# The expert layer: first products from rounded parts, biases in 128 rows, both batches in one program, weights fetched beside the attention

## The chip, the cores and the metric

The kernel is one program on one core of a Trainium2 chip. The core has a tensor engine (PE), a vector engine (DVE), a scalar engine (ACT), a general engine (POOL) and a sync engine that issues most DMAs (SP). The metric is the time of one execution on the device in microseconds; the median of several executions counts.

## The reference, cut to what matters

x has two batches of 2048 tokens of 128 numbers. Four layers follow each other, each with a residual and a layer norm: a state space mixer, a layer quantised to four bits, an attention with 16 heads, and the experts. Only the last one changes in what it computes:

```
flat = hidden.reshape(T, 128)
weights = the two largest of softmax(flat @ router_w + router_b), zero elsewhere   # 8 experts
shared  = gelu(flat @ sw1 + sb1) @ sw2 + sb2                                       # 128 -> 256 -> 128
h1      = gelu(einsum('td,edh->teh', flat, rw1) + rb1)                             # all 8 experts, 256 wide
expert  = einsum('teh,ehd->ted', h1, rw2) + rb2
out     = layernorm(x + shared + einsum('ted,te->td', expert, weights))
```

Every expert is computed for every token, in fp32.

## The kernel before

`build` runs three phases one after the other: `phase1` (mixer and quantised layer), `phase2` (attention) and `phase3` (experts). Each phase reads its input from DRAM and writes it back (`x_mid`), and each goes over the two batches with a hardware loop, `nc.Fori`. Inside a phase the engines run programs of their own, written out in blocks and tied together by semaphores; every block ends with a barrier of all engines, which also clears the semaphores. The order of the work on each engine is the order of its instructions; no planner is involved.

**Attention.** Per batch: `attention_input` (load, layer norm, transpose; its SP program also fetches the weights of the first two pairs of heads), `attention_first` (keys, queries and values of the first pair, and the maxima of its scores), `attention_pairs` (the long part, 1024 units over both batches) and `attention_output`. Keys and queries are split into a main part in the rounded type fp32r and a rest, `rest = exact - main`. A score is the sum of three fp32r products (main x main, main x rest, rest x main, L1176) and a fourth that subtracts the row's maximum. These products are over 64 rows and come in pairs, one for each head of a pair, on the two halves of the array. The maxima come from L957, also fp32r; the product of probabilities and values, L1187, is fp32.

**Experts.** `phase3` has a first block that fetches the weights with 17 DMAs, nine from SP and eight from ACT (L1461, L1467), waits for them, and makes the table `order`. Then the loop over the batches begins. A batch is 4 chunks (`CHUNKS`) of 512 tokens, a chunk has 9 steps (`ALL`): 8 experts and the shared one. For step k:

- `up(k)` on PE (L1547): two products of 128x512, fp32. The profile shows each fp32 product as two records.
- ACT applies gelu with the bias of the first layer (L1603), twice per step, into `hid`.
- `down(k)` on PE (L1563): for each of four groups of 128 tokens two products with 128 columns. In the ninth step each group begins with one more product, `weightT` (the routing weights, transposed, 9 rows) times `down_b` (the 9 second biases, 9 rows), L1561.
- DVE multiplies by the token's routing weight into `part` (L1684), and POOL adds it to `mixed` (L1715).

PE issues `up(k + 1)` ahead of `down(k)`; both have two sets of PSUM banks. The preparation of the next chunk is spread over the steps of this one: the weights' transpose at step 2, x's transpose at step 3 (L1530) with ACT's copy at step 4 (L1590), the router's products at step 5 (L1538) followed by DVE's `bias`, and exp (L1594) and `choose` (about 17 small DVE operations, L1635 to L1651) at step 7. The layer norm of a chunk runs during the steps of the next: `centre`, `square_act`, `variance`, POOL's power, `scale`, and SP stores the result. In the first chunk of a batch, the load, transpose, router and `choose` come one after the other before the first step; after the last chunk the norm and the store stand alone.

Of the kernel before, what the change touches and what calls it, by code (L numbers as in the profile page):

```python
# [23 lines left out]
P = 128  # L24
# [36 lines left out]
class Phase:  # L61


    def __init__(self, nc):
        self.nc, self.ctx, self.sems = nc, ExitStack(), []
# [8 lines left out]
    def sbuf(self, name, shape, dt=F32):  # L74
        return self.ctx.enter_context(self.nc.sbuf_tensor(name, shape, dt))

    def sem(self, name):
        s = self.ctx.enter_context(self.nc.semaphore(name))
        self.sems.append(s)
        return s  # L80
# [105 lines left out]
def build(nc, ins, out):  # L186

    x_mid = [nc.dram_tensor(f"x_mid_{i}", (BATCH, SEQ, D), F32, kind="Internal").ap() for i in range(2)]
    with Phase(nc) as ph:
# [5 lines left out]
        made, copied = ph.sem("made"), ph.sem("copied")  # L195
# [17 lines left out]
        phase2(nc, ins, x_mid[0], x_mid[1], **shared)  # L213
        phase3(nc, ins, x_mid[1], out, **shared)
# [596 lines left out]
def phase2(nc, ins, x_in, x_out, ident, ident_bf, ones, exponent, psum):  # L811


    with Phase(nc) as ph:
# [28 lines left out]
        common = {k: x for k, x in locals().items() if k not in ("nc", "x_in", "x_out", "ins", "ph")}  # L843

        with Phase(nc) as su:
            zero_one = su.sbuf("zero_one", [P, 2])
            loaded, filled, constants, step = (su.sem(s) for s in ("loaded", "filled", "constants", "step"))
# [23 lines left out]
        with nc.Fori(0, BATCH) as b:  # L871
            attention_input(nc, ins, x_in, b, common)
            attention_first(nc, common)
            attention_pairs(nc, ins, common)
            attention_output(nc, x_in, x_out, b, common)


def attention_input(nc, ins, x_in, b, m):
# [3 lines left out]
    with Phase(nc) as su:  # L882
# [120 lines left out]
def attention_first(nc, m):  # L1003
# [3 lines left out]
    with Phase(nc) as su:  # L1007
# [13 lines left out]
        with nc.Block() as block:  # L1021
            @block.tensor
# [67 lines left out]
def attention_pairs(nc, ins, m):  # L1090
# [26 lines left out]
    with Phase(nc) as su:  # L1117
# [245 lines left out]
def attention_output(nc, x_in, x_out, b, m):  # L1363
# [3 lines left out]
    with Phase(nc) as su:  # L1367
# [62 lines left out]
def phase3(nc, ins, x_in, out, ident, ident_bf, ones, exponent, psum):  # L1430
# [3 lines left out]
    ALL = EXPERTS + 1  # L1434
    with Phase(nc) as ph:
        up_w = ph.sbuf("up_w", [P, ALL, HID])
        down_w = ph.sbuf("down_w", [P, ALL, HH, D])
        up_b = ph.sbuf("up_b", [P, ALL, HH])
        down_b = ph.sbuf("down_b", [ALL, D])
        router_w = ph.sbuf("router_w", [P, EXPERTS])  # L1440
        router_b = ph.sbuf("router_b", [P, EXPERTS])
        order = ph.sbuf("order", [P, EXPERTS])
        stat = ph.sbuf("stat3", [P, 4, TILES])
        with Phase(nc) as su:
            loaded, made = su.sem("loaded"), su.sem("order_made")
            order_i = su.sbuf("order_i", [P, EXPERTS], mybir.dt.int32)
            loads = [
                (up_w[:, 0:EXPERTS, :], ins["rw1"].rearrange("e d h -> d e h")),
                (up_w[:, EXPERTS, :], ins["sw1"]),
                (down_w[:, EXPERTS], ins["sw2"].rearrange("(k p) d -> p k d", p=P)),  # L1450
                (up_b[:, 0:EXPERTS, :], ins["rb1"].rearrange("p (e k) -> p e k", e=EXPERTS)),
                (up_b[:, EXPERTS, :], ins["sb1"]),
                (down_b[0:EXPERTS, :], ins["rb2"]), (down_b[EXPERTS:ALL, :], ins["sb2"]),
                (router_w[:], ins["router_w"]),
                (router_b[:], ins["router_b"].unsqueeze(0).to_broadcast([P, EXPERTS])),
            ] + [(down_w[:, e], ins["rw2"][e, :, :].rearrange("(k p) d -> p k d", p=P)) for e in range(EXPERTS)]
            with nc.Block() as block:
                @block.sync
                def _(sp):
                    for dst, src in loads[0::2]:  # L1460
                        sp.dma_start(dst, src).then_inc(loaded, 16)  # L1461
                    sp.wait_ge(loaded, 16 * len(loads))

                @block.scalar
                def _(act):
                    for dst, src in loads[1::2]:
                        act.dma_start(dst, src).then_inc(loaded, 16)  # L1467

                @block.gpsimd
                def _(pool):  # L1470
                    nc.gpsimd.iota(order_i[:], [[1, EXPERTS]], base=-EXPERTS, channel_multiplier=0).then_inc(made, 1)

                @block.vector
                def _(dve):
                    dve.wait_ge(made, 1)
                    nc.vector.tensor_copy(order[:], order_i[:]).then_inc(made, 1)
                    dve.wait_ge(made, 2)
            nc.all_engine_barrier(sems_to_clear=sem_range(su.sems))
# [10 lines left out]
        weightT = ph.sbuf("weightT", [ALL, 2, BANK])  # L1489
# [3 lines left out]
        steps = [(u, e) for u in range(CHUNKS) for e in range(ALL)]  # L1493
# [264 lines left out]
```

## Time and profile before

| | |
|---|---|
| median of 3 runs | 3840.64 us (3838.98 to 3842.27) |
| the profiled execution | 3842.64 us, its span 3840.9 us |
| busy share PE, DVE, ACT, POOL | 88%, 63%, 44%, 72% |
| instructions executed | 48142 |
| instruction queues q8, q14 | 150 packets and 2.46 MB, 79 packets and 0.65 MB |
| single operations: ACT table load, DVE subtraction of 128x512, POOL add | 1.28, 0.69, 1.27 us |
| attention | from about 755 to 3507 us |
| experts | from 3507 us to the end |

The times of the rows further below are microseconds from the start of the span. PE is the row of the products, PEld that of the weight loads beside them, SPq and ACTq are DMA issues. Products overlap in the array: a record's duration is longer than the distance to the next one, so the pace is read from starts, not from durations. A row with "x8" merges eight instructions that follow each other. "PEclk" is the granted clock of PE, 1.00 for 2.4 GHz and 0.50 for 1.2.

### The profile page before, as it was taken

How to read it: one execution, taken by the hardware profiler on the slowest of the kernel's cores; microseconds unless marked ns; L12 is line 12 of the kernel's file. 1: busy time of each engine (PE TensorE's matmuls, PEld its weight loads, DVE VectorE, ACT ScalarE, POOL GpSimd, SP SyncE). 2: the span in 40 equal slices, each digit the busy share in tenths (PEclk: the TensorE clock that was granted, in tenths of full speed). 3: DMA queues.
4: the chain of work that ended last, by engine and by line, in shares of the span. 5: the costliest groups of instructions: out<-in, count | busy, mean ns of one | idle time of the engine just before them, and what ended most of it. 6: DMA issues, size and time to landing. Idle time of an engine off the chain costs nothing. (4 is left out here: it accounts for less than half of the span.)

```text
span 3840.9 us, 48142 instructions
## 1 busy us (share of the span) xinstructions
PE 3385.8 (88%) x18865; PEld 1747.3 (45%) x18865; DVE 2400.9 (63%) x2741; ACT 1681.7 (44%) x2037; POOL 2763.9 (72%) x1152
## 2 busy tenths in 40 slices
PE   5674677289999999999998599999999999995988
PEld 2222222245554555545454245555454554553766
DVE  5998699766666666666662665666666666642534
ACT  4331433144444554544544254545444455452433
POOL 1783188148888888888898198888888888893322
PEclk9997799689999999999999799999999999997989
DMA  1330233000000000000000100000000000001000
GB/s 25 133 113 22 65 114 104 27 3 1 4 1 4 4 1 4 1 4 2 1 1 10 33 1 4 1 4 1 4 4 1 4 1 1 1 1 55 12 18 9
DMA packets 61543, 76.24 MB, mean 20 GB/s; under 512 B 7289, under 2 KB 48962, under 8 KB 61250
## 3 DMA queue, kind: packets, MB, share of 16 engines
q1 hardware_dynamic: 57826, 72.03, 5.8%
q8 instruction: 150, 2.46, 0.3%
q10 hardware_dynamic: 3488, 1.10, 0.1%
q14 instruction: 79, 0.65, 0.1%
HBM read 66.30 MB, written 6.82 MB: 19 GB/s over the span
## 5 line engine op out<-in xcount | busy, mean ns | idle before, releaser
L1297 POOL TENSOR_TENSOR den_g<-den_g,p 128x1024 f32<-128x1024 f32 x896 | 2128.7, 2376 | 288.7 <-ACT p L1273 183.5
L964 DVE TENSOR_REDUCE quarters<-psum 128x2 f32<-128x1024 f32 x1024 | 1250.5, 1224 | 938.8 <-PE psum L957 935.7
L1273 ACT ACTIVATE p<-psum 128x1024 f32<-128x1024 f32 x1024 | 995.0, 1023 | 724.5 <-PE psum L1176 716.5
L1187 PE MATMUL psum<-p,v 128*64 128x512 f32 x4096 | 991.3, 605 | 0.0
L957 PE MATMUL psum<-k_main,q_main 64*128 64x512 f32 x2048 | 462.2, 446 | 13.7 <-DVE quarters L964 11.2
L1187 PEld LDWEIGHTS psum<-p,v 128*64 128x64 f32 x4096 | 248.5, 136 | 469.4 <-issue 315.6
L1176 PE MATMUL psum<-q_main,k_main 64*128 64x512 f32 x2048 | 407.5, 394 | 4.5 <-PEq L1087 4.5
L1176 PE MATMUL psum<-q_rest,k_main 64*128 64x512 f32 x2048 | 404.4, 390 | 0.0
L1176 PE MATMUL psum<-q_main,k_rest 64*128 64x512 f32 x2048 | 404.3, 390 | 0.0
L1176 PE MATMUL psum<-row_shift,row_ones 64*128 64x512 f32 x2048 | 403.8, 389 | 0.0
L957 PEld LDWEIGHTS psum<-k_main,q_main 64*128 64x128 f32 x2048 | 193.3, 184 | 362.5 <-issue 198.7
L712 POOL TENSOR_TENSOR seen<-state,c_sb 128x2048 f32<-128x2048 f32 x64 | 291.3, 4552 | 76.6 <-DVE state L661 76.0
L598 PE MATMUL psum<-seen,ident 128*128 128x512 f32 x512 | 259.4, 642 | 15.7 <-POOL seen L712 14.2
L1176 PEld LDWEIGHTS psum<-q_main,k_rest 64*128 64x128 f32 x2048 | 193.9, 185 | 43.6
L1176 PEld LDWEIGHTS psum<-row_shift,row_ones 64*128 64x128 f32 x2048 | 194.0, 185 | 43.1
L1176 PEld LDWEIGHTS psum<-q_main,k_main 64*128 64x128 f32 x2048 | 194.1, 186 | 42.8 <-issue 11.3
L1176 PEld LDWEIGHTS psum<-q_rest,k_main 64*128 64x128 f32 x2048 | 194.0, 185 | 42.6
L1297 POOL TENSOR_TENSOR den_g<-p 128x1024 f32<-128x1024 f32 x64 | 151.0, 2359 | 55.0 <-ACT p L1273 52.7
L701 POOL TENSOR_TENSOR xnT<-dx,work 128x1024 f32<-128x1024 f32 x32 | 75.2, 2351 | 154.3 <-DMA work<-bc_rows 154.3
L586 PE MATMUL psum<-bc,pick 64*128 64x512 f32 x192 | 72.7, 461 | 122.0 <-DVE state L661 118.2
L1715 POOL TENSOR_TENSOR mixed<-mixed,part 128x512 f32<-128x512 f32 x56 | 70.8, 1265 | 129.3 <-DVE part L1684 129.3
L1603 ACT ACTIVATE hid<-psum,up_b 128x512 f32<-128x512 f32 x144 | 91.1, 683 | 156.1 <-PE psum L1547 156.1
(242 smaller groups left out, 3291.0 us busy)
## 6 DMA issues: line engine op xcount, KB each, us to landing
c_sb<-bc_rows SPq DMA_DIRECT2D x64, 512.0 KB, 3.5
work<-bc_rows SPq DMA_DIRECT2D x32, 512.0 KB, 4.8
resid<-in_resid SPq DMA_DIRECT2D x8, 256.0 KB, 3.6
x_mid<-resid SPq DMA_DIRECT2D x8, 256.0 KB, 2.6
xa<-x_mid SPq DMA_DIRECT2D x8, 256.0 KB, 3.8
x_tok<-x_mid SPq DMA_DIRECT2D x8, 256.0 KB, 3.5
x_mid<-x_tok SPq DMA_DIRECT2D x8, 256.0 KB, 2.6
x<-x_mid SPq DMA_DIRECT2D x8, 256.0 KB, 2.8
```

Of the source, the lines that this page charges most:

```text
L586: last = nc.tensor.matmul(in_psum(h)[:, k * BANK:(k + 1) * BANK], pick[:, n, :], bc[:, at:at + BANK], start=True, stop=True)
L598: last = nc.tensor.matmul(y_sum[:, h, k * BANK:(k + 1) * BANK], ident[:], seen[:, i % SLOTS, h, k * BANK:(k + 1) * BANK], start=(n == 0), ...
L701: nc.gpsimd.tensor_tensor(fed[:, k % SLOTS, :], dx[:, 1, s * SCAN:(s + 1) * SCAN], b_sb[:, k % SLOTS, :], ALU.mult).then_inc(fed_by_pool, 1)
L712: nc.gpsimd.tensor_tensor(seen[:, i % SLOTS], state[:, i % SLOTS], c_sb[:, i % C_SLOTS, :].unsqueeze(1).to_broadcast([P, EH, SCAN]), ALU.m ...
L957: last = nc.tensor.matmul(max_banks[:, piece(h)], q[hi(h), c * BANK + j * P:c * BANK + (j + 1) * P], k[hi(h), piece(quarter)], start=True, ...
L964: return nc.vector.reduce_max(quarters[:, :, n], max_banks.rearrange("p (h k) -> p h k", h=2), X_AXIS)
L1176: last = nc.tensor.matmul(s_bank(u)[:, piece(h)], left[hi(h)], right[hi(h)], start=(i == 0), stop=(i == len(terms) - 1))
L1187: last = nc.tensor.matmul(o_bank[hi(h), :], vv[:, kt, hi(h)], p[:, u % LIVE, h, :], start=(kt == 0), stop=(kt == KT - 1))
L1273: nc.scalar.activation(flat(p[:, u % LIVE]), s_bank(u), ACT.Exp, scale=float(DH) ** -0.5).then_inc(p_ready, 1)
L1297: nc.gpsimd.tensor_tensor(sums, first, src, ALU.add).then_inc(added_g, 1)
L1603: nc.scalar.activation(hid[:, k % 2, h, :], up_bank(k)[:, h * BANK:(h + 1) * BANK], ACT.Gelu, bias=up_b[:, e, h:h + 1]).then_inc(hid_ready, 1)
L1715: nc.gpsimd.tensor_tensor(mixed[:, u % 2], x[:, u % 2] if e == 0 else mixed[:, u % 2], part[:, e % 2], ALU.add).then_inc(summed, 1)
```

## The change

Four things change, all but the third in how `phase3` does its work.

1. `up` uses rounded parts: `up_main` and `x_main` in fp32r, `up_rest` and `x_rest` the differences to the exact values, and three products for each one: main x main, main x rest, rest x main. ACT makes the main parts (of the weights once, of x in each chunk, ahead of its copy of xT), DVE makes the rests. The transposed x stays in fp32 for the router.
2. `weightT` and `down_b` get 128 rows, the upper 119 of them zero, so the bias product is over 128 rows. POOL clears both once.
3. `phase2`'s loop over batches becomes a Python loop: the program holds the attention twice. `phase3`'s becomes one run over 8 chunks (`GROUPS`), so that the second batch's first chunk is prepared like any other.
4. The expert weights live in tiles allocated ahead of `phase2`, and SP issues all 17 loads in `attention_first` of the first batch. `phase3`'s first block goes; `order` is made inside the main block.

```diff
         phase1(nc, ins, x_mid[0], **shared)
-        phase2(nc, ins, x_mid[0], x_mid[1], **shared)
-        phase3(nc, ins, x_mid[1], out, **shared)
+        with Phase(nc) as late:
+            experts = expert_weights(late, ins, experts_loaded)
+            phase2(nc, ins, x_mid[0], x_mid[1], experts, **shared)
+            phase3(nc, ins, x_mid[1], out, experts, **shared)
...
+                @block.gpsimd
+                def _(pool):
+                    nc.gpsimd.memset(experts["down_b"][:], 0.0).then_inc(cleared, 1)
+                    pool.wait_ge(cleared, 1)
...
-        with nc.Fori(0, BATCH) as b:
+        for b in range(BATCH):
             attention_input(nc, ins, x_in, b, common)
-            attention_first(nc, common)
-            attention_pairs(nc, ins, common)
+            attention_first(nc, b, common, experts if b == 0 else None)
+            attention_pairs(nc, ins, b, common)
             attention_output(nc, x_in, x_out, b, common)
...
+            if experts is not None:
+                @block.sync
+                def _(sp):
+                    for dst, src in experts["loads"]:
+                        sp.dma_start(dst, src).then_inc(experts["loaded"], 16)
...
+        up_main = ph.sbuf("up_main", [P, ALL, HID], F32R)
+        up_rest = ph.sbuf("up_rest", [P, ALL, HID], F32R)
+        x_main = ph.sbuf("x3_main", [P, 2, BANK], F32R)
+        x_rest = ph.sbuf("x3_rest", [P, 2, BANK], F32R)
-        weightT = ph.sbuf("weightT", [ALL, 2, BANK])
+        weightT = ph.sbuf("weightT", [P, 2, BANK])
-        steps = [(u, e) for u in range(CHUNKS) for e in range(ALL)]
-        with nc.Fori(0, BATCH) as b, Phase(nc) as su:
+        steps = [(u, e) for u in range(GROUPS) for e in range(ALL)]
+        with Phase(nc) as su:
...
+                        if u == 0:
+                            pe.wait_ge(main_ready, e + 1)
+                            pe.wait_ge(rest_ready, e + 1)
+                        if e == 0:
+                            pe.wait_ge(split, u + 1)
+                            pe.wait_ge(x_split, u + 1)
                         for h in range(HH):
-                            last = nc.tensor.matmul(up_bank(k)[:, h * BANK:(h + 1) * BANK], up_w[:, e, h * P:(h + 1) * P],
-                                                    xT[:, u % 2], start=True, stop=True)
+                            cols = slice(h * P, (h + 1) * P)
+                            terms = ((up_main, x_main), (up_main, x_rest), (up_rest, x_main))
+                            for i, (left, right) in enumerate(terms):
+                                last = nc.tensor.matmul(up_bank(k)[:, h * BANK:(h + 1) * BANK], left[:, e, cols], right[:, u % 2],
+                                                        start=(i == 0), stop=(i == len(terms) - 1))
                         last.then_inc(up_psum, 1)
...
                     turn_x(0)
+                    pe.wait_ge(weights_loaded, 16 * len(loads))
                     route(0)
                     up(0)
...
+                        nc.scalar.copy(x_main[:, u % 2], turn_bank).then_inc(split, 1)
                         nc.scalar.copy(xT[:, u % 2], turn_bank).then_inc(turned_sb, 1)
...
+                    act.wait_ge(weights_loaded, 16 * len(loads))
+                    for e in range(3):
+                        nc.scalar.copy(up_main[:, e, :], up_w[:, e, :]).then_inc(main_ready, 1)
                     copy_x(0)
                     share(0)
+                    for e in range(3, ALL):
+                        nc.scalar.copy(up_main[:, e, :], up_w[:, e, :]).then_inc(main_ready, 1)
...
+                    rest_of_weights(0, 3)
+                    rest_of_x(0)
                     bias(0)
                     choose(0)
+                    rest_of_weights(3, ALL)
...
+                        if e == X_TURN_AT + 1 and u + 1 < GROUPS:
+                            rest_of_x(u + 1)
...
+                    nc.gpsimd.iota(order_i[:], [[1, EXPERTS]], base=-EXPERTS, channel_multiplier=0).then_inc(order_made, 2)
+                    nc.gpsimd.memset(weightT[:], 0.0).then_inc(cleared, 1)
```

`rest_of_x` is one DVE subtraction of 128x512, `rest_of_weights` one of 128x256 per expert, each into an fp32r tile. A trailing tag on the names in the attention's functions keeps the tiles and semaphores of the two copies apart.

## Rows read from the trace of the kernel before

**Rows 1.** The windows by stage: length, busy time of each engine (records), PEclk, DMA share, GB/s.
```profile
3692.00:3831.00 139.00, 138.84 (x798) 100.73 (x796) 56.70 (x129) 57.42 (x89) 43.52 (x35) 1.00 0.03 10
...
3507.00:3526.00 19.00, 3.38 (x13) 2.92 (x14) 0.54 (x5) 1.87 (x2) 0.14 (x1) 0.50 0.55 153
```

**Rows 2.** The chain that ended last, second batch: start, length, engine, what was written, line.
```profile
3692.66 1.78 PE psum L1563 x16
3694.44 1.72 PE psum L1547 x4
...
3699.67 0.44 PE psum L1576 x4
...
3711.05 0.79 PE psum L1538 x8
...
3722.46 0.41 PE psum L1561 x2
3722.87 0.64 PE psum L1563 x4
```

**Rows 3.** Timeline of PE in the attention: start, length, engine, line, operation, shapes; half clock first.
```profile
814.84 0.66 PE L1176 MATMUL psum<-q_main,k_rest 64*128 64x512 f32 x2
815.27 0.66 PE L1176 MATMUL psum<-row_shift,row_ones 64*128 64x512 f32 x2
...
3404.23 0.39 PE L1176 MATMUL psum<-row_shift,row_ones 64*128 64x512 f32 x2
3404.46 0.40 PE L957 MATMUL psum<-k_main,q_main 64*128 64x512 f32 x2
3404.79 1.94 PE L1187 MATMUL psum<-p,v 128*64 128x512 f32 x8
3406.66 0.50 PE L957 MATMUL psum<-k_main,q_main 64*128 64x512 f32 x2
```

**Rows 4.** Timeline between the batches of the experts: last `down` and first `down`.
```profile
3667.98 0.71 PE L1563 MATMUL psum<-down_w,hid 128*128 128x128 f32 x4
...
3692.49 1.95 PE L1563 MATMUL psum<-down_w,hid 128*128 128x128 f32 x16
```

**Rows 5.** Timeline from the attention's end to the first `down`.
```profile
3507.13 0.39 SPq L1461 DMA_DIRECT2D up_w<-in_rw  x1
...
3519.16 15.89 SPq L1507 DMA_DIRECT2D x<-x_mid  x3
...
3521.95 1.11 PE L1530 MATMUL psum<-ident,x 128*128 128x128 f32 x4 [30.21 <-DMA x<-x_mid]
3523.10 0.58 ACT L1590 COPY x3T<-psum 128x512 f32<-128x512 f32 x1 [2.84 <-PE psum L1530]
...
3523.73 1.88 PE L1538 MATMUL psum<-router_w,x3T 128*128 128x8 f32 x8 [0.67 <-ACT x3T L1590]
...
3526.40 0.23 ACT L1594 ACTIVATE probs<-probs 128x32 f32<-128x32 f32 x1 [2.72 <-DVE probs L1630]
...
3530.35 1.95 PE L1563 MATMUL psum<-down_w,hid 128*128 128x128 f32 x16
```

**Rows 6.** Timeline of `attention_input`, first and second batch: issue of xa, first DVE work.
```profile
759.15 2.08 SPq L890 DMA_DIRECT2D xa<-x_mid  x4
...
765.13 3.19 DVE L104 BATCH_NORM_STATS2 six<-xa 128x6 f32<-128x128 f32 x16 [7.81 <-DMA xa<-x_mid]
...
2132.07 3.31 SPq L890 DMA_DIRECT2D xa<-x_mid  x4
...
2140.39 3.19 DVE L104 BATCH_NORM_STATS2 six<-xa 128x6 f32<-128x128 f32 x16 [13.90 <-DMA xa<-x_mid]
```

**Rows 7.** Timeline around the eighth and ninth step of a chunk.
```profile
3557.46 1.26 ACT L1603 ACTIVATE hid<-psum,up_b 128x512 f32<-128x512 f32 x2
...
3560.24 0.48 PE L1561 MATMUL psum<-down_b,weightT 9*128 9x128 f32 x2
...
3564.62 0.69 DVE L1687 TENSOR_TENSOR mixed<-mixed,psum 128x512 f32<-128x512 f32 x1 [0.57 <-PE psum L1563]
```

More of the change, by code:

```diff
@@ L842, in phase2 @@
         newt = ph.sbuf("newt", [P, BANK])
-        common = {k: x for k, x in locals().items() if k not in ("nc", "x_in", "x_out", "ins", "ph")}
+        common = {k: x for k, x in locals().items() if k not in ("nc", "x_in", "x_out", "ins", "ph", "experts")}
         with Phase(nc) as su:
             zero_one = su.sbuf("zero_one", [P, 2])
-            loaded, filled, constants, step = (su.sem(s) for s in ("loaded", "filled", "constants", "step"))
+            loaded, filled, cleared, step = (su.sem(s) for s in ("loaded", "filled", "cleared", "step"))
             with nc.Block() as block:
@@ L881, in attention_input @@
         m[k] for k in "xaT attnT stat six two gamma beta psum ident w_qkv w_o".split())
-    with Phase(nc) as su:
+    with Phase(nc, f"_{b}") as su:
         xa = su.sbuf("xa", [P, TILES, D])
@@ L1115, in attention_pairs @@
     adds = KT - 1
-    with Phase(nc) as su:
+    with Phase(nc, f"_{b}") as su:
         p = su.sbuf("p", [P, LIVE, 2, BANK])
@@ new lines, with expert_weights @@
+GROUPS = BATCH * CHUNKS
+def expert_weights(ph, ins, loaded):
+    up_w = ph.sbuf("up_w", [P, ALL, HID])
+    down_w = ph.sbuf("down_w", [P, ALL, HH, D])
+    up_b = ph.sbuf("up_b", [P, ALL, HH])
+    down_b = ph.sbuf("down_b", [P, D])
+    router_w = ph.sbuf("router_w", [P, EXPERTS])
+    router_b = ph.sbuf("router_b", [P, EXPERTS])
+    loads = [
+        (up_w[:, 0:EXPERTS, :], ins["rw1"].rearrange("e d h -> d e h")),
+        (up_w[:, EXPERTS, :], ins["sw1"]),
+        (down_w[:, EXPERTS], ins["sw2"].rearrange("(k p) d -> p k d", p=P)),
+        (up_b[:, 0:EXPERTS, :], ins["rb1"].rearrange("p (e k) -> p e k", e=EXPERTS)),
+        (up_b[:, EXPERTS, :], ins["sb1"]),
+        (down_b[0:EXPERTS, :], ins["rb2"]), (down_b[EXPERTS:ALL, :], ins["sb2"]),
+        (router_w[:], ins["router_w"]),
+        (router_b[:], ins["router_b"].unsqueeze(0).to_broadcast([P, EXPERTS])),
+    ] + [(down_w[:, e], ins["rw2"][e, :, :].rearrange("(k p) d -> p k d", p=P)) for e in range(EXPERTS)]
+    return locals()
@@ L1442, in phase3 @@
+def phase3(nc, ins, x_in, out, experts, ident, ident_bf, ones, exponent, psum):
+    up_w, down_w, up_b, down_b, router_w, router_b, loads, weights_loaded = (
+        experts[k] for k in "up_w down_w up_b down_b router_w router_b loads loaded".split())
+    with Phase(nc) as ph:
         order = ph.sbuf("order", [P, EXPERTS])
+        order_i = ph.sbuf("order_i", [P, EXPERTS], mybir.dt.int32)
+        up_main = ph.sbuf("up_main", [P, ALL, HID], F32R)
+        up_rest = ph.sbuf("up_rest", [P, ALL, HID], F32R)
@@ L1443, in phase3 @@
         stat = ph.sbuf("stat3", [P, 4, TILES])
[L1444 to L1478, printed above, removed]
@@ L1511, in _ @@
                     load(1)
-                    for u in range(CHUNKS):
-                        if u + 2 < CHUNKS:
+                    for u in range(GROUPS):
+                        if u + 2 < GROUPS:
                             sp.wait_ge(summed, EXPERTS * u + 1)
@@ L1671, in scale, with rest_of_x, rest_of_weights @@
                         nc.vector.tensor_tensor(mixed[:, u % 2], mixed[:, u % 2], spread(y, D), ALU.mult).then_inc(normed, 1)
+                    def rest_of_x(u):
+                        dve.wait_ge(split, u + 1)
+                        dve.wait_ge(turned_sb, u + 1)
+                        if u >= 2:
+                            dve.wait_ge(up_psum, ALL * (u - 1))
+                        nc.vector.tensor_tensor(x_rest[:, u % 2], xT[:, u % 2], x_main[:, u % 2].bitcast(F32),
+                                                ALU.subtract).then_inc(x_split, 1)
+                    def rest_of_weights(first, last):
+                        for e in range(first, last):
+                            dve.wait_ge(main_ready, e + 1)
+                            nc.vector.tensor_tensor(up_rest[:, e, :], up_w[:, e, :], up_main[:, e, :].bitcast(F32),
+                                                    ALU.subtract).then_inc(rest_ready, 1)
+                    dve.wait_ge(order_made, 2)
+                    nc.vector.tensor_copy(order[:], order_i[:]).then_inc(order_made, 1)
                     for u in range(2):
                         st.link(nc.vector.memset(weight[:, u, :, EXPERTS:ALL], 1.0))
+                    dve.wait_ge(order_made, 3)
+                    rest_of_weights(0, 3)
+                    rest_of_x(0)
                     bias(0)
                     choose(0)
+                    rest_of_weights(3, ALL)
                     for k, (u, e) in enumerate(steps):
```

65 lines of the change are left out of this document (30 added, 35 removed).

## The prediction

> **What bounds the kernel now.** I read the windows by stage first, because the change touches two stages with different limits. Almost all of it lies in the expert stage, from 3507 us to the end at 3840.9. In the second batch's run of experts PE is busy 138.84 of 139 us at full clock, and DVE, ACT and POOL are all under half; ahead of the first batch lies a stretch of 19 us in which PE does 3.4 us of work, at half clock [rows 1]. The chain that ended last says the same in order of time: through the second batch's steps it has nothing but PE pieces, each beginning where the last ended. One expert step is 1.72 us of `up` (L1547) and 1.78 of `down` (L1563); a turn of the weights or of x is 0.44, the router 0.79, and the ninth step is four groups of 0.41 (L1561, the biases) and 0.64 [rows 2]. So what shortens PE's work there shortens the span, microsecond for microsecond, as long as ACT and DVE keep up.
>
> **First products.** A chunk has 9 steps, a batch 4 chunks: 72 steps. In each, `up` has two products of 128x512, and each shows as two records, 0.43 us apart: 4 x 0.43 = 1.72. Each becomes three products of rounded (fp32r) operands, 6 records a step. No row shows an fp32r product over 128 rows. The nearest are the scores of the attention, fp32r over 64 rows, issued as pairs on the two halves of the array: a pair starts every 0.43 us in the stretch at half clock and every 0.23 at full clock (3404.23 to 3404.46) [rows 3]. 0.43 is 512 columns at 1.2 GHz, so these go one column a cycle, and at 2.4 GHz that is 0.213. A single 128-row record has one weight load where the pair has two, so I put it between 0.213 and 0.23: 0.22, a step's `up` at 1.32 us, 0.40 less. Two steps belong to the start (below); 70 x 0.40 = **28.0 us**, with ends of 30.8 (at 0.213) and 23.8 (at 0.23). The change also puts products of two number types next to each other (fp32r, then fp32) twice a step. No row has that alone. Where type and shape of the tile both change, the attention pays 0.10 to 0.15 on each side: 0.33 from the last fp32r pair to the p,v products instead of 0.23, and 1.87 until the next fp32r pair where four pairs of 0.43 are 1.72 [rows 3]. I take zero, since the tile shape explains it (next part), and keep 2 x 0.10 x 70 = 14 us as the other end.
>
> **Biases in 128 rows.** With 9 rows a group takes 1.05 us (0.41 + 0.64). Six records at the pace of the other steps (1.78 / 16 = 0.111) would be 0.67. The two bias records are no larger than the others, and the four behind them take 0.64 instead of 0.44: the loss is on both sides of the change from 9 rows to 128, not in the columns [rows 2]. With 128 rows everywhere I expect 0.67: 0.38 x 4 groups x 8 chunks = **12.2 us**. The ends are 0 and 12.2. The Trainium skill ("TensorE: Matmul & The Clock Gate", Why this matters for your kernels) says that a single product over 32 rows takes the same time as one over 128, by which this edit would be worth nothing. The Trainium skill ("TensorEngine Tiling (Array Packing)", Key Properties) also says that a change of the tiling mode drains the engine, and by that it would be worth the whole 12; the 0.41 and the 0.64 agree with the second. The clearing of `weightT` and `down_b` is one POOL memset each, while POOL waits for the first `part`: nothing.
>
> **Both batches in one program.** Now the last `down` of the first batch ends at 3668.69 and the first of the second at 3694.44, 25.75 us later. Between them stand the tail of the normalisation, its store, the barrier, the load of x, turn, router and two `up` at half clock [rows 4]. In steady running the same work costs one `down`, two `up`, a turn and a router: 1.78 + 3.44 + 0.44 + 0.79 = 6.45. Saved: **19.3 us** (18 to 20); the tail of the last batch stays.
>
> **Weights beside the attention, and the new start.** The attention's last block lets go at 3507.1, when the weight loads begin; x is asked for at 3519.16, and the first `down` starts at 3530.35: 23.2 us [rows 5]. After, x is asked for at 3507.1. I add up from there: 2.8 to landing, 1.1 turn, two ACT copies of 0.58 (x_main stands ahead of xT, so the router is 0.6 later than it was), 1.7 router, 0.8 biases and maximum on DVE, 0.25 exp: 3515.1. Then ACT has six copies of 128x256 before its first gelu. A 128x512 copy takes 0.58 and a 128x32 activation 0.23, so I estimate 0.40 plus a gap, 2.5 in all. A table load of 1.28 and the gelus of 1.26 follow: hid at about 3520.4. PE is ahead of this even at half clock: router until 3513.9, two `up` of six times 0.43 until 3519.1. So the first `down` starts at about 3520.5, 13.4 after the barrier: **9.8 us** less (7 to 11). The first three weight copies and a table load (2.6) are hidden by the 3.9 until x is turned, and DVE's rests (three beforehand, six of some 0.36 behind `choose`, until about 3521.7) come ahead of the `up` that reads them. On SP the 17 loads take about 8.5 us of issue in the first attention block, in which SP has nothing else to do; that block's PE and DVE work runs over 30 us, so the barrier does not wait for SP. The next DMAs queued behind them are the weights of a later pair, wanted tens of microseconds later. If that cover were gone it would cost at most those 8.5 us.
>
> **Attention unrolled.** Its instructions are the same. The second batch's xa is read by DVE 8.3 us after the first issue, the first batch's 6.0 after it; the loop's back edge is one explanation [rows 6]. I take **1.5 us**, between 0 and 3. Code fetch: the instruction queues moved 2.46 + 0.65 MB in 229 packets; over 48142 instructions that is 65 bytes each, so the loop bodies were already fetched anew for every batch and the longer program fetches no more (both queues are in the table of time and profile).
>
> **What is late next.** A step of PE becomes 3.10 us. ACT has two gelus (1.26); its tightest place is the eighth expert, with two table loads and an exp between gelus: there hid is ready at 3558.72 and `down` starts at 3560.24, 1.5 early [rows 7]. From that gelu's predecessor to this `down` PE has two steps, less 0.9 after: still 0.6 early. The extra copy (0.58) is in another step, with 0.7 to spare. DVE's longest piece is `choose`: it ends 0.57 before DVE is wanted for the ninth `down` [rows 7]; with that `down` coming 0.8 earlier for two shorter `up` and 1.5 for its bias groups, it ends about 1.7 after it. PE wants that PSUM bank only two `down`s later, so about 2 us of slack remain. `rest_of_x` (0.69, up to 2 when POOL's add of 1.27 holds it) falls in a step in which DVE otherwise has 0.69 of work. POOL has one add a step. I take no new wait.
>
> **Sum.** 28.0 + 12.2 + 19.3 + 9.8 + 1.5 = 70.8 us. The profiled execution was 3842.64 us (span 3840.9): 3772. The runs' median lies 2.0 lower, so I forecast **3770 us**.
>
> **Rivals.**
> - *The full-array rounded product takes two passes* (0.43 us, like an fp32 record now). Then `up` is 2.58, +0.86 x 70 = +60; the first `down` comes at about 3524 (gain 6), and with 12.2, 19.3 and 1.5 the net is +21: 3862, slower. It decides from a pace of about 0.38 us on. For it: no row of 128 rows in this type. Against it: the pairs' pace at both clocks. 4%.
> - *Changing number type stalls PE* at each border of `up` and `down`: +14, 3784 (to 3798 at twice the price). For it: the attention's switches, where type changes too [rows 3]. Against: the bias groups pay as much with no change of type. 12%.
> - *The bias group stays at 1.05*, since something other than its row count makes it slow (its operands, or the order of its records): +12, 3782. Against it: the four `down` records behind each pair pay too. 6%. The rule of the Trainium skill on small products ("TensorE: Matmul & The Clock Gate", Why this matters for your kernels) would make this of the time.
> - *DVE or ACT becomes late in the last steps of a chunk* by a microsecond or so: +8, 3778. For it: `choose` passes the end of `down`. 8%.
> - My forecast, with its own range of 3761 to 3778: 70%.
>
> **Numbers.** From 3760 (pace 0.213, attention 3, start 11) to 3791, which takes in two of the middle rivals in part. A difference under 0.2% (about 8 us) is what a measurement of this kernel cannot tell from none. Only the first rival gives slower: 5% with surprises in the attention; 1% for the same; 94% faster.
>
> **What would show it.** In the profile after: 432 `up` records with starts 0.22 apart, a step of 3.1; a ninth step of 1.3 + 2.7 with 12 groups merged at 0.111; no gap near 3640; the first `down` 13.4 us after the attention's last barrier; ACT and DVE still waiting for PE in nearly every step; PE idle for ACT or DVE would show the fourth rival. A step over 3.3, or an attention longer by more than 3 us, would make the forecast wrong.

## The result, and the profile after

The changed kernel takes 3775.16 us (median of 4, 3772.75 to 3776.89) against 3840.42 before: a ratio of 0.983, 95% interval 0.9819 to 0.9842. The forecast was 3770, its range 3760 to 3791. The profiled execution took 3775.72 us with a span of 3773.7; that of before 3842.64 and 3840.9. The two spans differ by 67.2 us. The expert stage, from the attention's last barrier to the end, went from 333.8 to 268.7 us, which is 65.1 of it. The other 2.1 lie ahead of that stage.

The chain that ended last, in the changed kernel: start, length, engine, what was written, line (L1560 is `up`, L1577 `down`, L1591 and L1534 the turns, L1542 the router).

```profile
3540.78 1.39 PE psum L1560 x6
3542.17 1.78 PE psum L1577 x16
3543.95 1.38 PE psum L1560 x6
3545.56 0.45 PE psum L1577 x4
3546.23 0.45 PE psum L1577 x4
3546.90 0.45 PE psum L1577 x4
3547.57 0.45 PE psum L1577 x4
3548.01 1.39 PE psum L1560 x6
3549.40 1.78 PE psum L1577 x16
...
3554.35 1.38 PE psum L1560 x6
3555.73 0.44 PE psum L1591 x4
```

Set beside [rows 2], `up` is 1.385 us instead of 1.72, `down` is unchanged, and the four groups of the ninth step follow each other every 0.67 us instead of every 1.05. The chain still has nothing but PE in it, through all eight chunks.

The windows of the start, the steady part and the end: length, busy time of PE, its loads, DVE, ACT and POOL (records), PEclk, DMA share, GB/s.

```profile
3505.00:3518.00 13.00, 7.96 (x25) 6.18 (x25) 7.17 (x30) 6.82 (x16) 1.03 (x2) 0.54 0.15 42
3518.00:3761.00 243.00, 243.00 (x1730) 223.49 (x1731) 128.73 (x299) 123.87 (x192) 90.13 (x70) 1.00 0.05 15
3761.00:3774.00 13.00, 2.67 (x24) 2.48 (x23) 5.13 (x12) 0.63 (x1) 2.28 (x2) 0.69 0.07 20
```

PE is busy 243 of 243 us where [rows 1] had one batch at a time, and the hole between the batches [rows 4] is gone. Who waited for whom from 3518 us to the end: engine, what it wrote, releaser, total us, times, longest.

```profile
POOL mixed L1763 <- DVE part L1728: 164.9, 64, 14.8
ACT hid L1624 <- PE psum L1560: 109.3, 56, 2.8
DVE part L1728 <- PE psum L1577: 106.9, 57, 2.9
ACT work L146 <- DVE mixed L1681: 13.5, 8, 5.6
...
DVE mixed L1731 <- PE psum L1577: 2.0, 1, 2.0
...
PEld psum L1577 <- ACT hid L1624: 0.9, 1, 0.9
...
PE psum L1577 <- ACT hid L1624: 0.5, 1, 0.5
```

ACT and DVE wait for PE, and PE waited for another engine once in this stretch, 0.5 us at the first `down`. The row of L1731 shows what "What is late next" said: DVE comes to the ninth `down` too late to wait for it in seven chunks of eight (before the change it had waited in each, 8 times for 10.5 us in all), and PE does not wait for DVE.

The start, timeline of the changed kernel, against [rows 5].

```profile
3504.99 17.55 SPq L1511 DMA_DIRECT2D x<-x_mid  x3
3505.01 1.02 ACT L1614 CAST up_main<-up_w 128x256 fp32r<-128x256 f32 x3 [4.00 <-PEq L1441]
...
3508.32 1.12 PE L1534 MATMUL psum<-ident,x 128*128 128x128 f32 x4 [18.30 <-DMA x<-x_mid]
3509.48 0.58 ACT L1605 CAST x_main<-psum 128x512 fp32r<-128x512 f32 x1 [3.45 <-PE psum L1534]
...
3510.69 1.85 PE L1542 MATMUL psum<-router_w,x3T 128*128 128x8 f32 x8 [1.25 <-ACT x3T L1606]
...
3513.38 1.93 ACT L1618 CAST up_main<-up_w 128x256 fp32r<-128x256 f32 x6
...
3515.33 1.28 ACT L1624 ACT_TABLE_LOAD   x1
...
3517.94 2.05 PE L1577 MATMUL psum<-down_w,hid 128*128 128x128 f32 x16 [0.46 <-ACT hid L1624]
```

The first `down` comes 12.95 us after the barrier (the stage's first DMA) instead of 23.2, by the path that was added up: x, turn, two copies, router, exp, six weight copies, table load, gelu.

### The profile page after: what moved, and what is told of

The parts are those of the page before. It is cut to its first block and busy times, and to the rows that moved or that the text cites. A ratio compares the mean times of both kernels' runs of the same rounds, so it can differ in the third digit from the quotient of the medians.

```text
span 3773.7 us, 48349 instructions
## 1 busy us (share of the span) xinstructions
PE 3348.8 (89%) x19009; PEld 1769.9 (47%) x19009; DVE 2411.6 (64%) x2756; ACT 1687.3 (45%) x2053; POOL 2768.3 (73%) x1154
## 3 DMA queue, kind: packets, MB, share of 16 engines
q8 instruction: 146, 2.39, 0.3%
## 5 line engine op out<-in xcount | busy, mean ns | idle before, releaser
L600 PE MATMUL psum<-seen,ident 128*128 128x512 f32 x512 | 261.6, 647 | 15.7 <-POOL seen L714 14.1
L600 PEld LDWEIGHTS psum<-seen,ident 128*128 128x128 f32 x512 | 94.7, 200 | 138.5 <-issue 102.4
L626 ACT ACTIVATE psum<-delta,decay 128x1024 f32<-128x1024 f32 x32 | 35.8, 1118 | 268.3 <-DVE state L663 268.3
```

The lines of the kernel that those rows point to most:

```text
L600: last = nc.tensor.matmul(y_sum[:, h, k * BANK:(k + 1) * BANK], ident[:], seen[:, i % SLOTS, h, k * BANK:(k + 1) * BANK], start=(n == 0), ...
```

## Experiments

All edits are to the changed kernel. The medians carry some noise of their own: in kernels whose attention is the same instruction for instruction, the expert stage begins anywhere between 3500.65 and 3505.97 us in the profiles. So each experiment is read twice, by its median and by the length of the expert stage in its profile, from the first DMA after the attention's last barrier to the end of the span (268.7 in the changed kernel). The kernel before was measured again beside each set of runs, at 3840.40, 3840.62 and 3839.38 us, so the sets can be compared.

The stage's length has a spread too, and it lies in one place. Its parts, in us: from the issue of x to its turn on PE, from there to the first `down`, and from there to the end.

| | x to turn | turn to first `down` | first `down` to end |
|---|---|---|---|
| before | 2.79 | 8.40 | 310.55 |
| changed | 3.33 | 9.62 | 255.76 |
| first products in fp32 | 2.79 | 10.44 | 278.92 |
| nine rows | 2.85 | 9.62 | 268.11 |
| weights fetched late | 3.47 | 9.61 | 255.65 |
| one block for each batch | 2.75 | 9.62 | 273.97 |
| attention as a loop | 2.81 | 9.62 | 255.50 |
| bf16 parts | 2.67 | 9.61 | 249.33 |
| halves of 256 columns | 2.74 | 9.62 | 259.04 |
| copies first, ten products | 11.74 | 6.45 | 255.74 |
| copies first | 2.73 | 9.33 | 255.96 |
| copies first, two products | 3.59 | 6.92 | 255.70 |
| this start and bf16 | 3.60 | 6.91 | 249.39 |

(Before, and where the weights are fetched late, x is only asked for 12.03 and 12.24 us into the stage.) Where nothing in the start differs, the way from the turn to the first `down` repeats within 0.01 us, but x took 3.33 us in the changed kernel's profile and 2.67 to 2.85 in the seven others that ask for it at once and have no products ahead of its turn. Some 0.5 us of its 268.7 and 12.95 is therefore chance, and a difference in the stage should be read by the part that the edit touches.

**First products in fp32 again.**

```diff
-                            terms = ((up_main, x_main), (up_main, x_rest), (up_rest, x_main))
+                            terms = ((up_w, xT),)
```

> The first products go back to one fp32 product of up_w and xT each; the rounded parts are still made on ACT and DVE but not read by PE. Theory (PE paces every step, and the three rounded products save 1.72 - 1.385 = 0.335 us in each of 70 steps): 23.5 us slower than the changed kernel, 3799, and the four `up` records of a step 0.43 apart again. Rival (part of the gain of the rounded products was eaten by ACT or DVE, which would now have more room): less than 20 us slower, with PE idle for hid or for a PSUM bank somewhere in the changed kernel's steps.

3795.67 us (3794.71 to 3801.23), 20.5 more; the stage is 3792.8 - 3500.65 = 292.15 us, 23.4 more, where the theory had 23.5. Its chain:

```profile
3551.74 1.78 PE psum L1577 x16
3553.53 1.72 PE psum L1560 x4
```

From the first `down` to the end it is 23.2 us more, 0.331 for each of the 70 steps, against 0.335 from the records. So the rounded products are worth 23.2 us there, and no gain was lost to ACT or DVE. (In the start, at half clock, fp32 costs 0.8 us more, and x landed 0.5 earlier.) The median is 3 below the forecast for it; it doesn't decide, since the stage of this profile began 4.3 us earlier.

**Nine rows again.**

```diff
-                                nc.tensor.matmul(dst, weightT[:, u % 2, j * P:(j + 1) * P], down_b[:], start=True, stop=False)
+                                nc.tensor.matmul(dst, weightT[0:ALL, u % 2, j * P:(j + 1) * P], down_b[0:ALL, :], start=True, stop=False)
```

> The bias product again reads 9 rows of weightT and down_b, nothing else changes. Theory (going from 9 rows to 128 and back costs about 0.1 us at each border of the pair): the group of four tokens' tiles goes from 0.67 back to 1.05 us, 32 groups, 12.3 us slower than the changed kernel, 3787.5. Rival (a product over few rows takes as long as one over 128, and the slow groups came from the order of the records or their operands): within 2 us of 3775.

3785.05 us (3783.85 to 3786.26), 9.9 more; the stage is 3783.7 - 3503.12 = 280.6, 11.9 more, and from the first `down` to the end 12.35, or 0.386 for each of the 32 groups. Its groups in the chain:

```profile
3543.50 0.64 PE psum L1577 x4
3544.56 0.64 PE psum L1577 x4
```

They are 1.06 us apart, as before the change, with the same operands, order and records: only the number of rows differs. The rival that the bias group stays slow is out. The Trainium skill ("TensorE: Matmul & The Clock Gate", Why this matters for your kernels) says that a single product over 32 rows takes as long as one over 128. Here the pair over 9 rows, between products of 128 rows, costs about 0.19 us on either side of it, and the measurement decides. The Trainium skill ("TensorEngine Tiling (Array Packing)", Key Properties) also says that a change of the tiling mode drains TensorE; the trace agrees with that, at this price.

**Weights fetched at the start of the expert stage.**

```diff
-                    for dst, src in experts["loads"]:
-                        sp.dma_start(dst, src).then_inc(experts["loaded"], 16)
+                    pass
...
+        with nc.Block() as block:
+            @block.sync
+            def _(sp):
+                for dst, src in loads[0::2]:
+                    sp.dma_start(dst, src).then_inc(weights_loaded, 16)
+                sp.wait_ge(weights_loaded, 16 * len(loads))
+
+            @block.scalar
+            def _(act):
+                for dst, src in loads[1::2]:
+                    act.dma_start(dst, src).then_inc(weights_loaded, 16)
+        nc.all_engine_barrier()
```

> The 17 weight loads move from the attention to a block of their own at the start of the expert stage (nine on SP, eight on ACT, then a barrier), as before the change. Theory (the loads and their barrier took 12.0 us in the kernel before, all of it on the path, and the second start with its weight copies costs the changed kernel 2 of them): 3787, with x asked for about 12 us after the attention's last barrier and the attention as long as now. Rival (the loads beside the attention cost something there, on SP or in the memory): the attention gets shorter by what they cost, and the total rises by less than 10.

3782.83 us (3780.81 to 3786.31), 7.7 more; the stage is 3782.0 - 3501.03 = 281.0, 12.3 more. x is asked for 12.24 us after the first weight load. The two readings differ by 4.6 us, and the stage of this profile begins at 3501.03, 4 us earlier than in the changed kernel. That looks like the rival, loads that cost the attention something; but the first kernel above has those loads and begins the stage at 3500.65, the second at 3503.12. The block with the loads settles it, from its first product to the next block's, in the changed kernel and then without the loads:

```profile
776.51 5.96 PE L997 MATMUL psum<-xaT,w_qkv 128*128 128x512 f32 x10 [2.04 <-PEq L930]
...
810.82 0.80 PE L1190 MATMUL psum<-q_main,k_main 64*128 64x512 f32 x2 [2.25 <-PEq L1101]
```

```profile
775.11 7.35 PE L997 MATMUL psum<-xaT,w_qkv 128*128 128x512 f32 x10 [2.04 <-PEq L930]
...
810.81 0.80 PE L1189 MATMUL psum<-q_main,k_main 64*128 64x512 f32 x2 [2.25 <-PEq L1100]
```

The block takes 34.31 us with the loads and 35.70 without. All of the difference is in its first ten products (5.96 and 7.35): the rest is 28.35 in both. So the loads cost this block nothing, and the rival is out; the 12.3 us in the stage are what the fetch there costs. The ten products also explain part of the attention's spread. In the 26 executions of this block in all profiles they take between 4.53 and 7.58 us, with and without loads, and the rest 28.33 to 28.36. The difference is when PE's clock rises: from 776 to 780 us the granted clock is 0.58 in the changed kernel and 0.50 here.

**One block for each batch.**

```diff
+        for half in range(BATCH):
+            with Phase(nc, f"_{half}") as su:
...
-                        sp.dma_start(x[:, u % 2], tokens(x_in, u // CHUNKS, u % CHUNKS)).then_inc(loaded, 16)
+                            sp.dma_start(x[:, u % 2], tokens(x_in, half, u)).then_inc(loaded, 16)
...
-                        if u == 0:
+                            if u == 0 and half == 0:
```

> The expert stage becomes two blocks of four chunks again, one for each batch, written out and not looped; the weights are split only in the first. Theory (between the batches stood tail, store, barrier, load, turn, router and two `up` at half clock): a gap comes back in which the first `down` of the second batch ends about 25 us after the last of the first, against 5.8 in steady running; 19 us slower, 3794. Rival (a good part of the old gap was the hardware loop's back edge): clearly less than 17 us slower.

3791.82 us (3787.28 to 3793.04), 16.7 more; the stage is 3790.2 - 3503.86 = 286.3, 17.6 more. The last group of the first batch and the first `down` of the second in its timeline:

```profile
3636.64 0.61 PE L1578 MATMUL psum<-down_w,hid 128*128 128x128 f32 x4
...
3659.24 2.21 PE L1578 MATMUL psum<-down_w,hid 128*128 128x128 f32 x16
```

From end to end this is 24.2 us, against 25.75 with the hardware loop [rows 4]. Steady running needs 5.8 for the same work, so 18.4 us is the price of going dry once, without any loop; from the first `down` of the first batch to the end the profile has 18.2 more. Of the 1.5 us between 24.2 and 25.75, 1.3 are the two `up` at half clock, 5.26 us here against 6.55 with fp32. x lands in 2.59 instead of 3.45 us and is asked for 0.3 sooner after the store, while ACT's second copy and the first `down` take 0.9 more. So the hardware loop's edge can account for 1.1 us of the old gap at most, and the rival is out.

**The attention as a hardware loop.**

```diff
-        for b in range(BATCH):
+        with nc.Fori(0, BATCH) as b:
             attention_input(nc, ins, x_in, b, common)
-            attention_first(nc, b, common, experts if b == 0 else None)
-            attention_pairs(nc, ins, b, common)
+            attention_first(nc, 0, common, experts)
+            attention_pairs(nc, ins, 0, common)
```

> The attention is a hardware loop over the batches again (the weights' loads are therefore issued in both batches). Theory (the loop's back edge costs the second batch's first load about 2 us): 3777, with the second batch's xa read by DVE about 8 us after its issue instead of 5.9. Rival (the 2.1 us by which the attention ended earlier is the spread between executions, 1.1 of it already there before the attention begins): within 1 us of 3775 and no change in that distance.

The loads are issued in both batches here, and the waits count both. 3775.91 us (3771.92 to 3776.95): no difference that the medians can tell. The second batch's first issue and first DVE work, with the loop and then in the changed kernel:

```profile
2131.45 3.58 SPq L897 DMA_DIRECT2D xa_i<-x_mid  x4
...
2140.17 3.19 DVE L104 BATCH_NORM_STATS2 six<-xa_i 128x6 f32<-128x128 f32 x16 [14.28 <-DMA xa_i<-x_mid]
```

```profile
2130.32 2.03 SPq L897 DMA_DIRECT2D xa<-x_mid  x4
...
2136.18 3.19 DVE L104 BATCH_NORM_STATS2 six<-xa 128x6 f32<-128x128 f32 x16 [11.17 <-DMA xa<-x_mid]
```

8.7 us with the loop, 5.9 without. The kernel before, also a loop, has 8.3, and the ten other profiles without it have 5.8 to 6.4, so this is the loop's edge; 1.3 to 1.6 of it are the four issues themselves (3.58 and 3.31 us against 2.03). Both theories are half right. The place is real, but the rest of the second batch varies as much from one execution to the next (in the changed kernel its 1368.8 us are the longest of all profiles, the others have 1364.1 to 1367.7), and the medians don't show it. The whole attention, from its first DMA to the stage's first, takes 2751.5 and 2749.9 us in the two profiles with the loop and 2745.8 to 2750.5, on average 2747.1, in the eleven without. That points to some 3 us that do reach the total, but two profiles are few.

**Parts in bf16**, less exact than fp32r.

```diff
-        up_main = ph.sbuf("up_main", [P, ALL, HID], F32R)
+        up_main = ph.sbuf("up_main", [P, ALL, HID], BF16)
```

and the same for `up_rest`, `x_main` and `x_rest`.

> The main parts and rests of the first products are bf16 instead of fp32r, so the first products are less exact; counts and shapes stay. Theory A (an fp32r record of 512 columns costs 0.018 us more than 512 cycles because of its four-byte type): records 0.216 apart, `up` 1.30, 6 us faster than the changed kernel, 3769. Theory B (every record with its weight load costs that much): 0.23 stays, 3775.

3767.41 us (3766.24 to 3771.66), 7.8 less; the stage is 3764.9 - 3503.29 = 261.6, 7.1 less, of which 6.4 behind the first `down` and 0.7 x's landing. Its `up`:

```profile
3601.76 0.38 PE L1560 MATMUL psum<-x_rest,up_main 128*128 128x512 bf16 x1
3601.97 0.38 PE L1560 MATMUL psum<-x_main,up_rest 128*128 128x512 bf16 x1
3602.19 0.38 PE L1560 MATMUL psum<-x_main,up_main 128*128 128x512 bf16 x1
```

0.2155 apart, theory A. The Trainium skill ("TensorE: Matmul & The Clock Gate", Part 1) gives a start-to-start distance of N / 2.4 + 2.5 ns at full clock, an estimate of 216 ns for 512 columns: with bf16 the trace agrees, with fp32r it is 15 ns more. The record of a weight load gets shorter with the type as well, 0.19 us to 0.10; the next experiment separates the two.

**Halves of 256 columns**, fp32r.

```diff
+                            for q in range(2):
                                 for i, (left, right) in enumerate(terms):
-                                    last = nc.tensor.matmul(... h * BANK:(h + 1) * BANK], left[:, e, cols], right[:, u % 2],
+                                    last = nc.tensor.matmul(... h * BANK + q * HALF:h * BANK + (q + 1) * HALF], left[:, e, cols],
+                                                            right[:, u % 2, q * HALF:(q + 1) * HALF],
```

> Each rounded product of 512 columns becomes two of 256, twice the records and weight loads, the same columns. Three accounts of the pace of 0.23: the weight load of the next record (0.19 long) is what a record waits for: 256 columns are no faster, `up` 2.76 a step, +96 us, 3871. A fixed 0.018 per record beside the columns: 12 x (0.107 + 0.018) = 1.50, +8 us, 3783. The columns themselves go slower than one a cycle in this type: 1.39 as now, 3775.

3774.74 us (3772.79 to 3777.8), as before the edit; the stage is 3775.7 - 3504.30 = 271.4, 2.7 more, and behind the first `down` 3.3 more. In steady running and, below, in the start at half clock:

```profile
3603.35 0.28 PE L1562 MATMUL psum<-x_rest,up_main 128*128 128x256 f32 x1
3603.47 0.28 PE L1562 MATMUL psum<-x_main,up_rest 128*128 128x256 f32 x1
3603.59 0.28 PE L1562 MATMUL psum<-x_main,up_main 128*128 128x256 f32 x1
```

```profile
3513.17 0.41 PE L1562 MATMUL psum<-x_main,up_main 128*128 128x256 f32 x1
3513.39 0.41 PE L1562 MATMUL psum<-x_rest,up_main 128*128 128x256 f32 x1
```

0.119 apart for 256 columns and 0.231 for 512: 0.112 for the 256 more (0.438 ns a column, where 2.4 GHz is 0.417), and some 0.007 fixed. So the third account is nearest, the weight load is out (it would have made 256 columns no faster than 512), and the fixed part is less than half of what the second had. At half clock it is 0.213 for 256, one column a cycle: in these rows the four-byte type loses time only at full clock.

**Another start: ten products to warm PE.**

```diff
-                    for e in range(3):
+                    for e in range(ALL):
                         nc.scalar.copy(up_main[:, e, :], up_w[:, e, :]).then_inc(main_ready, 1)
...
-                    rest_of_weights(0, 3)
+                    rest_of_weights(0, ALL)
...
+                    for i in range(10):
+                        nc.tensor.matmul(banks(psum, 5), ident[:], ones[:].unsqueeze(1).to_broadcast([P, TPC, P]), start=True, stop=True)
                     turn_x(0)
```

> All nine weight copies on ACT and all nine rests on DVE come before x is split, where ACT idles 3.45 us, and PE does ten fp32 products of 512 columns on constants while x is loaded, written to a bank that is overwritten later. Theory (the start is bound by ACT's six copies behind exp, and next by PE at half clock): router and two `up` run at full clock, 0.8 and 2.8 us instead of 1.9 and 5.1, the first `down` comes about 3 us earlier, 3772. Rival (the clock doesn't rise in time, or falls again while PE waits for x): 0.5 us earlier, since `up` of the second step still ends at 12.4.

3780.66 us (3778.01 to 3782.07), 5.5 more: a miss of both. I had not added up the price of the ten: 20 records, 11.85 us, where x takes 2.7 to 3.3 to land. The first `down` came 18.2 us after the barrier. But the windows show what it was tried for, the granted clock (column before the last two):

```profile
3510.00:3512.00 2.00, 2.00 (x3) 0.67 (x2) 0.34 (x2) 0.00 (x0) 0.00 (x0) 0.50 0.13 37
3512.00:3514.00 2.00, 2.00 (x6) 0.92 (x5) 0.00 (x0) 0.00 (x0) 0.00 (x0) 0.97 0.31 94
```

PE had been busy without a gap from 3506.02 when its clock rose from 1.2 to 2.4 GHz at 3512, and router and `up` then ran at full clock: from the turn to the first `down` it is 6.45 us instead of 9.62.

**The copies first, without warming.** The same edit with no products.

> Only the order at the start changes: all nine weight copies (3 us on ACT) and all nine rests (3.1 us on DVE) come before x arrives; no warm-up products. Theory (PE at half clock is next behind ACT's six copies): the two first `up` run as before and the first `down` comes when the second ends, 0.4 to 0.5 us earlier after the attention's last barrier than the 12.95 of the changed kernel; the total is the same within its spread, 3774 to 3775. Rival (the six copies cost their whole 1.9 us): 1.9 earlier.

3772.63 us (3768.93 to 3776.68), 2.5 less, which the ranges don't separate; the first `down` is 12.06 us after the barrier, 0.9 earlier. But 0.6 of that is x's landing, and from the turn to the first `down` only 0.3 is gained. ACT had been the last to be waited for by no more than that; PE at half clock is next, as the theory had it.

**The copies first, two products.** `range(2)` instead of `range(10)`.

> As e9_copies_first, and PE does two fp32 products of 512 columns on constants (four records, 0.85 each at half clock, 3.4 us) while x is loaded. With ten of them PE was still busy 8 us after x had landed, and its clock had risen 6 us after it began. Theory (what cost time in e8_start was their number alone): x is turned at most 0.3 us later than without them, the clock rises about 6 us after the barrier, ahead of most of the two `up`, and the first `down` comes about 11 us after the barrier, 1.8 less than in the changed kernel: 3773. Rival (the 1.2 us in which PE waits for ACT's two copies of x keep the clock down): the first `down` at 12.5, as in e9_copies_first.

3770.66 us (3769.32 to 3771.56), 4.5 less; the first `down` is 10.51 us after the barrier. That is 2.4 earlier than in the changed kernel's profile, and 1.8 to 2.0 earlier than the 12.3 to 12.5 of the profiles with the same start in which x landed as usual. The theory, 1.8, holds. Its start:

```profile
3501.89 15.18 SPq L1511 DMA_DIRECT2D x<-x_mid  x3
...
3501.94 3.75 PE L1582 MATMUL psum<-ones,ident 128*128 128x512 f32 x4 [15.45 <-PEq L1441]
3505.48 1.06 PE L1534 MATMUL psum<-ident,x 128*128 128x128 f32 x4
...
3507.80 1.03 PE L1542 MATMUL psum<-router_w,x3T 128*128 128x8 f32 x8 [1.25 <-ACT x3T L1608]
...
3512.40 2.05 PE L1577 MATMUL psum<-down_w,hid 128*128 128x128 f32 x16 [0.71 <-ACT hid L1624]
```

The router takes 1.03 instead of 1.85 and two `up` 2.8 instead of 5.1; now `down` waits 0.7 for hid, so the start is bound by exp, table load and gelu on ACT. The two products still hold the turn of x back by some 0.8 us (3.59 instead of 2.67 to 2.85). PE's wait of 1.25 us for x3T did not keep the clock down, as the window behind it shows:

```profile
3507.00:3509.00 2.00, 1.21 (x10) 1.19 (x11) 0.83 (x2) 0.65 (x2) 0.00 (x0) 0.98 0.08 24
```

**Everything that helped, together**: this start and the bf16 parts.

> The version that the runs point to: the start of e10_short_warm and the bf16 parts of e6_bf16_parts, whose first products are less exact. Theory (the two gains add): 1.8 us less than e6_bf16_parts, 3765.5. Rival (the start is bound by ACT and DVE, not by PE, as soon as the records are shorter): the same as e6_bf16_parts, 3767.

3764.73 us (3764.36 to 3765.69), ratio to the kernel before 0.9804 (0.9791 to 0.9818); the stage is 3762.6 - 3502.70 = 259.9 us. The gains add, part by part: behind the first `down` 6.4 less, as with bf16 alone, and the first `down` at 10.51, as with this start alone. It beats both kernels, the changed one by 10.4 us in the medians and 8.8 in the stage. With fp32r parts the start alone gives 4.5 and 2.5. Some 0.5 of each stage figure is the late x in the changed kernel's profile.

## Why the prediction was right

The direction and the mechanism held, and the sum nearly: 70.8 us were forecast against the profiled execution, 66.9 came. The largest part of the difference is one term, the first products.

- **What bounds the stage.** PE's chain, before and after. In the first experiment the time behind the first `down` grew by 0.331 us for each of the 70 steps, and the records of `up` by 0.335, so each microsecond of PE was a microsecond of the stage.
- **First products, 28.0.** This term was mis-sized: it was 23.4 by the records (23.2 by the profile). The step that failed is the choice of 0.22, made because a single record has one weight load where the pair has two. The pace is 0.231, the pairs' own, and the number of weight loads does not set it: half as many columns with twice the loads run at nearly the same pace per column, and two bytes instead of four give 0.2155. The slow end of the prediction's range (23.8, from 0.23) was the right reading of [rows 3].
- **Changing the number type** costs nothing that the trace shows. `down` keeps its 1.78, and `up` is six times the 0.231 seen inside a step. The rows that spoke for that rival, the attention's switches, change the tile's shape too, and the second experiment shows that a change of shape alone costs about 0.19 us at each border.
- **Biases, 12.2.** A group takes 0.67, and the nine rows cost 12.35 us. The two borders of the shape were the cause, shown by changing the rows alone.
- **Both batches, 19.3.** Going dry costs 18.4 at the new pace of `up` and without the loop. The change gained 54.8 us behind the first `down`; without the 23.2 of the products and the 12.35 of the biases 19.3 are left for this term.
- **Weights and start, 9.8.** It was 10.3. The path was right and its sum came out by some luck: x took 3.3 us to land and not 2.8, the six copies took 1.9 and not 2.5, and the prediction's own terms up to the gelu's end add up to 12.85 us, not to the 13.3 that it took. With x as in the other profiles the gain would have been 10.8. Of the 12.03 us of the fetch, 1.2 go to the longer way from the turn to the first `down` and 0.5 to x.
- **Attention, 1.5.** It was 2.1 in the profile, 1.1 of it already there where the attention had not begun; that the two agree is luck. The loop's edge is worth 2.5 to 2.8 us at its place; that it reaches the total isn't shown, though the lengths of the attention point that way. The longer program fetched no more instructions: 2.39 + 0.61 MB on q8 and q14, against 2.46 + 0.65.
- **What is late next.** Nothing, for the reasons given. DVE came too late for the ninth `down` as worked out (by 1.4 us at the middle of the stage, where 1.7 was forecast), and PE's second bank hid it.

What stays open: why a four-byte operand takes 0.438 ns a column at full clock, and how much of the loop's edge reaches the total.

## What to carry to other kernels

When one engine is busy for a whole stage, count its records and read their distance from the nearest rows; take the pace of the nearest row as it is, and don't talk it down with a mechanism that no row shows. A small product in a stream of full ones is not small: filling it with zeros to the shape of its neighbours gave 12 us for two memsets. And a pipeline that is emptied between batches pays for its refill at half clock: keep it running, and where it must start anew, idle work for PE about as long as the first load can help: two products brought the first `down` 1.6 us nearer than the same start without them, while ten put it 6.1 further away. And when executions differ by more than the effect, split the profile where the edit acts: the way from the turn to the first `down` repeated within 0.01 us, while executions of one kernel differed by several.

## What was not expected of the hardware

At full clock fp32r operands come in at 0.231 us for 512 columns and 0.119 for 256, bf16 at 0.2155; at half clock both sizes of fp32r go one column a cycle (0.427 and 0.213). When PE's clock rises differs much from start to start. It was 6.0 us after PE had become continuously busy with the ten products. It was between 4.6 and 5.9 after the first product with two of them, and PE was idle for 1.25 us in that time, waiting for the transposed x. It was some 8.5 in the changed kernel and near 10 with the copies first, both with that same wait. In the attention the same ten products take anything from 4.53 to 7.58 us for that reason, and this is up to 3 us of a batch.
